# First layer of a graph network: one chunk's weighing, sums, product and statistics in one turn, and the layer's join in the same block

## The chip, the core and the metric

The kernel runs on one core of a Trainium2 chip. The metric is device time in microseconds (us), median of three runs. Engines are named as in the profile: PE (matrix products), DVE (vector), ACT (activations), POOL (here it issues the gathers), SP (issues the plain transfers). Each works through its own instructions in order and waits on semaphores for the others.

## The reference

Four graph layers follow each other on 50,000 nodes of 128 features. The change is in the first one:

```python
h = x @ W
norm = dinv[src] * dinv[dst]              # with loops added, dinv = rsqrt(degree)
out = segment_sum(h[src] * norm[:, None], dst) + b
out = layer_norm(out) * ln_gamma + ln_beta
x = _layernorm(x + relu(out))             # what the next layer starts from
```

The kernel sums the weighted rows of `x` first and multiplies the sum by `W` afterwards. The edges are sorted by `dst`, so that a node's sum is a run along the edges; the runs that cross from one partition into the next are mended at the end, in the join.

## The kernel before

The padded edges lie in 128 partitions; a chunk is 7 columns of them (7 rows of 128 features in each partition), and there are 56 chunks (`k.NB`). A chunk passes through these steps:

- `load` on SP brings its records; `fetch` (L1436) on POOL issues 14 gathers, two for each column, which bring the target's own row (`in`, `own` in the code) and the source's row (`both`).
- `weigh` (L1454) on ACT: 14 scaled copies into `run` and `summed`.
- `edges` (L1469) on DVE: 7 chained steps that carry the run along the columns (L1475), then 7 steps that add the run to `summed` (L1477).
- PE turns `summed` (L1067), ACT copies the turned rows (L1108), PE multiplies by `W` onto the bias (L1073, L1079), ACT copies the product into `z` (L1116). This goes in two groups, of 4 and 3 columns (`GROUPS`).
- `stats` on DVE: mean and variance of `z` (L780 to L776); `first.log` on ACT: Ln and Exp (L790, L792), a first guess of the inverse root; `first.root` on DVE: one Newton step (L799 to L803); `first.apply` on ACT: `z` to `y` (L811).
- `residual` (L1498) on DVE: gain, bias, relu and the row of `x` (L1501 to L1503), then the statistics of `y`; `second.log`, `second.root`, and on ACT `apply_second` (L1507), which writes two tables' rows (`out`, 14 activations, all on L811). SP stores them (L1044), and stores `run` as well (`keep`, L1481).

`Flow.run` (L1021) writes the instructions out chunk by chunk: on every engine a turn goes through a list of steps, and each step has a lag, the number of chunks by which it runs ahead of the turn's own chunk. On DVE the list is `edges` 3 ahead, `stats` 0, `residual` 1 behind, `first.root` 0, `second.root` 1 behind. On ACT it is `weigh` 4 ahead, `apply_second` 2 behind, the product of the chunk 1 ahead, both `log`, `first.apply` 0, and the copies of turned rows. POOL fetches 4 ahead and SP loads 5 ahead of the turn and stores 3 behind. All loops are written out, none runs on the chip. Before the first chunk's sums, DVE prepares the later layers' weights (`side.vector`).

After the 56 chunks this block ends with a barrier of all engines, and a second block does the join: POOL gathers three small tiles (L1546 to L1549), then one chain of sums, product and three row norms runs through DVE, PE, ACT and POOL (`RowNorm`, L1171), and POOL writes the result into both tables (L1554). Then the next layer starts.

Of the kernel before, what the change touches and what calls it, by code (L numbers as in the profile page):

```python
# [11 lines left out]
I32 = mybir.dt.int32  # L12
# [5 lines left out]
D = 128  # L18
# [1145 lines left out]
class RowNorm:  # L1164
# [9 lines left out]
    def run(self, dve, step, v, o):  # L1174
        step(dve.bn_stats(out=self.raw[:], in_=v))  # L1175
        step(dve.bn_aggr(out=self.mv[:], in_=self.raw[:]))  # L1176
        step(dve.tensor_scalar(self.mv[:, 1:2], self.mv[:, 1:2], self.eps, None, ALU.add))  # L1177
        dve.nop().then_inc(self.asked, 1)
        dve.wait_ge(self.rooted, 1)
        step(dve.tensor_scalar(o, v, self.mv[:, 0:1], self.mv[:, 1:2], ALU.subtract, ALU.mult))  # L1180
# [225 lines left out]
def gcn(k):  # L1406
# [3 lines left out]
    with ExitStack() as c:  # L1410
# [58 lines left out]
        def edges(dve, step, c):  # L1469
# [17 lines left out]

        def kept(sp):
            for u in range(RING):
                sp.wait_ge(put_out[u], k.NB // RING * 16)  # L1490
            for u in range(UB):
                sp.wait_ge(src_out[u], k.TN * 16)
# [14 lines left out]
        def apply_second(act, c):  # L1507
            n.wait_stored(act, c)
            act.wait_ge(src_out[c.slot(UB)], (c.use(UB) + 1) * 16)
            second.apply(act, c, R(y, c), R(n.o[0], c))  # L1510
            second.apply_twice(act, c, R(y, c), R(n.o[1], c))

        side = Prepare(k, c, [n.p_t[0][0], n.p_t[1][0], *n.p_m], [y, n.z, n.o[0]])

        def begin(dve):
            side.vector(dve)
            step = Chain(dve, begun)
            step(dve.memset(run[:, RING - 1, J - 1, :], 0.0))

            step(dve.memset(n.o[1][:, :, :, 0:1], 1.0))  # L1520

        n.z_free = first.applied
        n.finished, n.freed = second.applied2, sem("freed")
        n.n_got = 2
# [15 lines left out]
        with nc.Block(no_gpsimd_drain=True) as b:  # L1540

            @b.gpsimd
# [1679 lines left out]
```

## Time and profile before

| | us |
|---|---|
| median of three runs (lowest, highest) | 6258.33 (6258.26, 6266.45) |
| span of the profiled execution, first to last instruction | 6250.9 |
| what the median has over that span | 7.4 |
| the 56 chunks' first gather on POOL, last gather | 356.17, 1373.04 |
| first instruction of the join's block | 1467.26 |
| first DVE instruction of the next layer | 1488.74 |

The page gives the profiled execution's span and no other time of its own; where a time of the whole is needed, the 7.4 us between span and median stand for what lies around it. Busy shares over the whole span (PE 73%, DVE 85%, ACT 75%, POOL 61%) are means over all four layers; the first one covers about 356 to 1489 us, and only that stretch matters here.

A row of a timeline gives the start, the length, the engine, the line of the kernel, the operation, what is written and read, the count where rows are merged, and in brackets the idle time of the engine ahead of it and who ended it. Instructions of one engine overlap: the next one may start before the last has ended.

### The profile page before, as it was taken

The numbers are of one execution on the slowest core, as the hardware profiler recorded it, in microseconds if no ns is written. First come the engines' busy times: TensorE is split into PE (matmuls) and PEld (weight loads), VectorE is DVE, ScalarE is ACT, GpSimd is POOL, SyncE is SP. The second block draws the span as 40 slices with busy tenths as digits, with TensorE's granted clock in tenths as the row PEclk, the third lists the DMA queues.
The fourth block names the chain that finished last, engine by engine and source line by source line (L and its number), as shares of the span: only waits on it lengthen the run. The fifth ranks groups of instructions, "written<-read, shape, count | busy, mean of one in ns | idle before, by whom it ended". The sixth has DMA issues, their size and how long they took to land. (4 is left out here: it accounts for less than half of the span.)

```text
span 6250.9 us, 117617 instructions
## 1 busy us (share of the span) xinstructions
PE 4548.2 (73%) x28601; PEld 3543.8 (57%) x28601; DVE 5315.0 (85%) x27201; ACT 4686.9 (75%) x14259; POOL 3804.5 (61%) x3880
## 2 busy tenths in 40 slices
PE   4143333333999979999979999949996769888881
PEld 2022222222888868888856777636654557666661
DVE  8767777774999978999969999957767859999996
ACT  7017888884999978999959999945545648888884
POOL 3057777763777737666366666447753445777774
PEclk9555555556999989999989999979998989999995
DMA  9377555553888845666547676646657954444441
GB/s 191 45 66 134 133 125 133 130 126 102 240 246 248 244 156 189 206 216 205 183 144 206 198 206 203 177 143 205 208 173 255 299 179 152 151 163 152 156 158 42
DMA packets 608007, 1075.90 MB, mean 172 GB/s; under 512 B 263700, under 2 KB 370015, under 8 KB 607193
## 3 DMA queue, kind: packets, MB, share of 16 engines
q1 hardware_dynamic: 476056, 787.63, 39.5%
q0 software_dynamic: 129920, 280.46, 20.6%
q8 instruction: 231, 3.78, 0.3%
q14 instruction: 456, 3.73, 0.2%
q10 hardware_dynamic: 1344, 0.30, 0.0%
HBM read 564.38 MB, written 530.59 MB: 175 GB/s over the span
## 5 line engine op out<-in xcount | busy, mean ns | idle before, releaser
L1925 POOL DMA_INDIRECT xs<-tab,rec x1176 | 1156.7, 984 | 358.4 <-issue 318.2
L2049 ACT ACTIVATE st<-xs,cb 128x128 f32<-128x128 f32 x2352 | 814.5, 401 | 0.9 <-DVE cg L1639 0.9
L2173 DVE SCALAR_TENSOR_TENSOR st<-st,cg 128x128 f32<-128x128 f32 x2352 | 719.5, 348 | 41.3 <-ACT st L2049 36.9
L1980 PE MATMUL p_y<-w_all,xt 128*128 128x258 f32 x2352 | 722.7, 390 | 30.6 <-DVE cA L2138 29.6
L2057 ACT ACTIVATE z<-p_a 128x384 f32<-128x384 f32 x1176 | 574.0, 488 | 119.3 <-PE p_a L1817 108.1
L1448 POOL DMA_INDIRECT in<-in_x,rec x392 | 388.0, 990 | 402.0 <-DMA rec<-meta 283.2
L2138 DVE CUSTOM_DVE_ANT_0 junk<-p_y,xs 128x129 f32<-128x129 f32 x2352 | 585.9, 288 | 11.4 <-PE p_y L1980 9.6
L1073 PE MATMUL p_m<-b_rows,ones_bf 3*128 3x512 bf16 x224 | 100.0, 446 | 648.3 <-ACT z L1116 648.3
L886 ACT ACTIVATE o<-y,norm 128x127 f32<-128x127 f32 (+1 forms) x1176 | 513.7, 488 | 6.8 <-DVE norm L880 6.7
L1817 PE MATMUL p_a<-ident,st 128*128 128x128 f32 x2352 | 468.1, 281 | 67.0 <-DVE st L2173 62.9
L2757 POOL DMA_INDIRECT xs<-res,rec x392 | 388.8, 992 | 198.8 <-issue 98.8
L2040 ACT ACTIVATE xt<-p_t 128x256 f32<-128x256 f32 (+1 forms) x1221 | 448.6, 368 | 79.5 <-PE p_t L1964 77.5
L1976 PE MATMUL p_a<-w_all,xt 128*128 128x128 f32 x2352 | 479.4, 286 | 27.1 <-ACT xt L2040 26.5
L2760 POOL DMA_INDIRECT out<-o,nodes x392 | 399.9, 1020 | 154.5 <-issue 118.5
L1997 PE MATMUL p_m<-w_all,xt 128*128 128x128 f32 x2352 | 489.4, 290 | 0.0
L1923 POOL DMA_INDIRECT xd<-tab,rec x336 | 338.1, 1006 | 231.5 <-DMA rec<-meta 155.9
L1141 POOL DMA_INDIRECT in<-tab,rec x392 | 390.8, 997 | 125.3 <-issue 119.2
L1817 PEld LDWEIGHTS p_a<-ident,st 128*128 128x128 f32 x2352 | 303.2, 141 | 272.5 <-DVE st L2173 189.9
L1821 PE MATMUL p_m<-w_all,z 128*128 128x128 f32 x2352 | 455.2, 275 | 0.1
L1822 PE MATMUL p_m<-w_all,z 128*128 128x128 f32 x2352 | 454.3, 274 | 0.0
L1073 PEld LDWEIGHTS p_m<-b_rows,ones_bf 3*128 3x128 bf16 x224 | 21.2, 95 | 710.1 <-ACT z L1116 691.2
L1452 POOL DMA_INDIRECT both<-x_info,rec x336 | 330.4, 983 | 102.4 <-issue 102.4
(778 smaller groups left out, 16334.5 us busy)
## 6 DMA issues: line engine op xcount, KB each, us to landing
states<-st SPq DMA_DIRECT2D x168, 910.0 KB
own<-tab SPq DMA_DIRECT2D x168, 448.0 KB
tab<-o SPq DMA_DIRECT2D x168, 448.0 KB
runs<-run SPq DMA_DIRECT2D x112, 448.0 KB, 6.8
tab<-out SPq DMA_DIRECT2D x112, 448.0 KB
x<-tab SPq DMA_DIRECT2D x112, 448.0 KB
xd<-tab SPq DMA_DIRECT2D x168, 192.0 KB, 3.5
angles<-st SPq DMA_DIRECT2D x56, 532.0 KB
```

Of the source, the lines that this page charges most:

```text
L886: ins = act.activation(o[:, r, skip:], v[:, r, skip:], ACT.Identity, bias=s[:, 1, r : r + 1], scale=s[:, 0, r : r + 1])
L1817: ins = pe.transpose(p_a[i][:, h * D : (h + 1) * D], halves(a)[:, h, :], k.ident[:])
L1821: pe.matmul(out_, a[:, 0:D], k.w_val[:, 0, :], start=False, stop=False)
L1822: return pe.matmul(out_, a[:, D : 2 * D], k.w_val[:, 1, :], start=False, stop=final)
L1925: pool.indirect_dma_start(xs[:, i, j, 0:D], None, table, bass.IndirectOffsetOnAxis(ap=rec[:, i, SRC, j : j + 1], axis=0)).then_inc(got_in[ ...
L1976: ins = pe.matmul(p_a[two(own_c, own_i)][:, 2 * D : 3 * D], xt[:, four(c, i), D : 2 * D], k.w_own[:, D : 2 * D], start=True, stop=True)
L1980: ins = pe.matmul(p_y[two(c, i)][:, 0 : H * X1], xt[:, four(c, i), 0:D], k.w_qk[:], start=True, stop=True)
L1997: pe.matmul(out_, xt[:, (four(c, j) + SCORE * J + 1) % 4, D : 2 * D], k.w_own[:, 0:D], start=False, stop=False)
L2049: ins = act.activation(state_of(r, j)[:, h, :], xs[:, c.slot(UB), j, 0:D], ACT.Copy, scale=co.b[:, c.slot(2), h, j : j + 1])
L2057: act.activation(z[:, c.slot(2), j, :], p_a[two(c, j)][:, 0 : 3 * D], ACT.Copy).then_inc(st_copied, 1)
L2138: ins = dve.tensor_tensor_reduce(junk[:, two(c, j), h], p_y[two(c, j)][:, h * X1 : (h + 1) * X1], xs[:, c.slot(UB), j, :], scale, 0.0, ALU ...
L2173: ins = dve.scalar_tensor_tensor(mine[:, h, :], prev[:, h, :], co.g[:, c.slot(2), h, j : j + 1], mine[:, h, :], ALU.mult, ALU.add)
```

## The change

The lags go. In turn i every engine handles chunk i up to its statistics, the residual of chunk i-1 and the second norm of chunk i-2; the instructions of the layer are written out for it in a block of its own, no longer through `Flow.run`. ACT weighs chunk i first in turn i and makes its Ln and Exp last in turn i. DVE takes the sums of chunk i, the residual of i-1, the statistics of i, then the roots of i-1 (second norm) and of i (first norm). The sums are handed to PE in the two groups. SP loads 5 ahead of the turn as before, but ahead of `keep`, and stores 2 behind. POOL issues all gathers in a row. The join's instructions stand in the same block: its two gathers that need no run follow the chunks' gathers, the gather of runs waits for the stores of `run`, the join's sums come ahead of the last residual on DVE, and its writes wait for the stores of both tables. The join uses three other banks.

```diff
     def run(self, dve, step, v, o):
+        self.ask(dve, step, v)
+        self.take(dve, step, v, o)
+
+    def ask(self, dve, step, v):
         step(dve.bn_stats(out=self.raw[:], in_=v))
         step(dve.bn_aggr(out=self.mv[:], in_=self.raw[:]))
         step(dve.tensor_scalar(self.mv[:, 1:2], self.mv[:, 1:2], self.eps, None, ALU.add))
         dve.nop().then_inc(self.asked, 1)
+
+    def take(self, dve, step, v, o):
         dve.wait_ge(self.rooted, 1)
         step(dve.tensor_scalar(o, v, self.mv[:, 0:1], self.mv[:, 1:2], ALU.subtract, ALU.mult))
...
             r = c.slot(RING)
             dve.wait_ge(weighted, c.count(1, 1))
-            for j in range(J):
-                prev = run[:, r, j - 1, :] if j else run[:, (r - 1) % RING, J - 1, :]
-                step(dve.scalar_tensor_tensor(run[:, r, j, :], prev, n.field(c, SAME)[:, j : j + 1], run[:, r, j, :], ALU.mult, ALU.add))
-            dve.nop().then_inc(edged, 1)
-            step(*[dve.scalar_tensor_tensor(summed[:, r, j, :], run[:, r, j, :], n.field(c, OWN1)[:, j : j + 1], summed[:, r, j, :],
-                                            ALU.mult, ALU.add) for j in range(J)])
-            dve.nop().then_inc(n.prepped, 1)
+            for a, z_ in GROUPS:
+                for j in range(a, z_):
+                    prev = run[:, r, j - 1, :] if j else run[:, (r - 1) % RING, J - 1, :]
+                    step(dve.scalar_tensor_tensor(run[:, r, j, :], prev, n.field(c, SAME)[:, j : j + 1], run[:, r, j, :], ALU.mult, ALU.add))
+                if z_ == J:
+                    dve.nop().then_inc(edged, 1)
+                step(*[dve.scalar_tensor_tensor(summed[:, r, j, :], run[:, r, j, :], n.field(c, OWN1)[:, j : j + 1], summed[:, r, j, :],
+                                                ALU.mult, ALU.add) for j in range(a, z_)])
+                dve.nop().then_inc(n.prepped, 1)
...
-        cut = 1
-        n.run([], [], [k.res, k.tab[1]], lambda c: [R(summed, c)], [k.w_skip],
-              [(3, edges), (0, stats), (-1, residual), (0, first.root), (-1, second.root)],
-              [(4, weigh), (-2, apply_second), (0, first.log), (-1, second.log), (0, lambda act, c: first.apply(act, c, R(n.z, c), R(y, c)))],
-              [], prep=True, sp_stages=[(1, keep)], begin=begin, sp_end=kept,
-              pe_begin=side.tensor, sp_after={-4: side.bring, UB - 1: side.put_away}, fetch=fetch, bring=bring, cut=cut)
+        n.n_got, n.n_out = 2, 2
+        outs = [k.res, k.tab[1]]
+        at = lambda i: Chunk(k, i // UB, i % UB)
...
-        cleared, fetched, joined, done, summed1 = [sem(x) for x in ("cleared", "fetched", "joined", "jdone", "summed1")]
+        cleared, hinted, fetched, joined, done, summed1 = [sem(x) for x in ("cleared", "hinted", "fetched", "joined", "jdone", "summed1")]
         turned1, copied1, made1, ready, put = [sem(x) for x in ("turned1", "copied1", "made1", "ready", "put")]
-        p_j, p_t, p_z = n.p_t[0][0], n.p_t[1][0], n.p_m[0]
+        p_j, p_t, p_z = side.sets[1][0:3]
...
+                for i in range(LEAD):
+                    load(at(i))
+                    if i == 1:
+                        side.bring(sp)
+                for i in range(k.NB + 2):
+                    if i + LEAD < k.NB:
+                        load(at(i + LEAD))
+                    if i < k.NB:
+                        keep(sp, at(i))
+                    if i == UB - 1:
+                        side.put_away(sp)
+                    if i >= 2:
+                        store(at(i - 2))
...
             @b.gpsimd
             def _(pool):
+                for i in range(k.NB):
+                    fetch(pool, at(i))
                 pool.memset(head[:], 0.0).then_inc(cleared, 1)
+                pool.indirect_dma_start(mine[:], None, A["x"], bass.IndirectOffsetOnAxis(ap=k.head_node[:], axis=0)).then_inc(hinted, 16)
+                pool.indirect_dma_start(hint[:].bitcast(I32), None, k.info, bass.IndirectOffsetOnAxis(ap=k.head_node[:], axis=0)).then_inc(hinted, 16)
                 pool.wait_ge(cleared, 1)
+                for u in range(RING):
+                    pool.wait_ge(put_out[u], k.NB // RING * 16)
                 pool.indirect_dma_start(head[:], None, k.runs, bass.IndirectOffsetOnAxis(ap=k.join_row[:], axis=0),
                                         bounds_check=k.NR - 1, oob_is_err=False).then_inc(fetched, 16)
-                pool.indirect_dma_start(mine[:], None, A["x"], bass.IndirectOffsetOnAxis(ap=k.head_node[:], axis=0)).then_inc(fetched, 16)
-                pool.indirect_dma_start(hint[:].bitcast(I32), None, k.info, bass.IndirectOffsetOnAxis(ap=k.head_node[:], axis=0)).then_inc(fetched, 16)
                 for norm in norms:
                     norm.root(pool)
                 pool.wait_ge(ready, 1)
+                for u in range(RING):
+                    pool.wait_ge(n.stored[u], k.NB // RING * 16 * n.n_out)
...
+                side.tensor(pe)
+                for i in range(k.NB):
+                    for g in range(NG):
+                        turn(at(i), g)
+                    for g in range(NG):
+                        product(at(i), g)
+
+                pe.wait_ge(edged, k.NB)
                 pe.matmul(p_j[:, 0:D], k.join_t[:], run[:, RING - 1, J - 1, :], start=True, stop=True).then_inc(joined, 1)
+                pe.matmul(p_z[:, 0:D], k.ones_bf[:], k.b_rows[:, 0, :], start=True, stop=False)
                 pe.wait_ge(summed1, 1)
                 pe.transpose(p_t[:, 0:D], o[:], k.ident[:]).then_inc(turned1, 1)
-                pe.matmul(p_z[:, 0:D], k.ones_bf[:], k.b_rows[:, 0, :], start=True, stop=False)
                 pe.wait_ge(copied1, 1)
                 pe.matmul(p_z[:, 0:D], ot[:], k.w_skip[:], start=False, stop=True).then_inc(made1, 1)
 
...
+                for i in range(k.NB + 2):
+                    c0, c1, c2 = at(i), at(i - 1), at(i - 2)
+                    if c0.there:
+                        weigh(act, c0)
+                    if c1.there:
+                        first.apply(act, c1, R(n.z, c1), R(y, c1))
+                    if c0.there:
+                        carry_turned(c0, 0)
+                    if c2.there:
+                        n.wait_stored(act, c2)
+                        act.wait_ge(src_out[c2.slot(UB)], (c2.use(UB) + 1) * 16)
+                        second.apply(act, c2, R(y, c2), R(n.o[0], c2))
+                    if c0.there:
+                        carry_turned(c0, 1)
+                        for g in range(NG):
+                            carry_product(c0, g)
+                    if i == k.NB:
+                        act.wait_ge(turned1, 1)
+                        act.activation(ot[:], p_t[:, 0:D], ACT.Copy).then_inc(copied1, 1)
+                    if c2.there:
+                        second.apply_twice(act, c2, R(y, c2), R(n.o[1], c2))
+                    if c1.there:
+                        second.log(act, c1)
+                    if c0.there:
+                        first.log(act, c0)
 
...
+                for i in range(k.NB):
+                    c0, c1 = at(i), at(i - 1)
+                    stage(s_edges, c0, edges)
+                    stage(s_residual, c1, residual)
+                    stage(s_stats, c0, stats)
+                    stage(s_second, c1, second.root)
+                    stage(s_first, c0, first.root)
+
                 step = Chain(dve, done)
-                dve.wait_ge(fetched, 48)
+                final = at(k.NB - 1)
+                dve.wait_ge(hinted, 32)
                 step(dve.tensor_scalar(o[:], mine[:], dinv, None, ALU.mult))
                 dve.wait_ge(joined, 1)
                 step(dve.tensor_tensor(o[:], o[:], p_j[:, 0:D], ALU.add))
+                dve.wait_ge(fetched, 16)
                 step(dve.tensor_tensor(o[:], o[:], head[:], ALU.add))
                 step(dve.tensor_scalar(o[:], o[:], dinv, None, ALU.mult))
                 dve.nop().then_inc(summed1, 1)
+                stage(s_residual, final, residual)
                 dve.wait_ge(made1, 1)
-                norms[0].run(dve, step, p_z[:, 0:D], z[:])
+                norms[0].ask(dve, step, p_z[:, 0:D])
+                stage(s_second, final, second.root)
+                norms[0].take(dve, step, p_z[:, 0:D], z[:])
```

On ACT, two turns of the program in the middle of the layer. Before, from the end of a weighing (`run`, `summed`) to the next weighing's first instruction; `out` is the second norm's result, `guess_208` and `guess_221` are the first and the second norm's, `xt` the turned rows:

```order
L1466 ACTIVATE summed<-in_160,rec 128x128
L811 ACTIVATE out_161<-y,norm_224 128x128 x7
L811 ACTIVATE out_162<-y,norm_224 128x127 x7
L1116 ACTIVATE z<-p_m_167 128x512
L1108 ACTIVATE xt<-p_t_165 128x512
L790 ACTIVATE guess_208<-rad_207 128x7
L792 ACTIVATE guess_208<-guess_208 128x7
L790 ACTIVATE guess_221<-rad_220 128x14
L792 ACTIVATE guess_221<-guess_221 128x14
L811 ACTIVATE y<-z,norm_211 128x128 x7
L1116 ACTIVATE z<-p_m_168 128x384
L1108 ACTIVATE xt<-p_t_166 128x384
```

Now, from the end of one chunk's weighing to the start of the next:

```order
L811 ACTIVATE y<-z,norm_211 128x128 x7
L1625 ACTIVATE xt<-p_t_165 128x512
L811 ACTIVATE out_161<-y,norm_224 128x128 x7
L1625 ACTIVATE xt<-p_t_166 128x384
L1632 ACTIVATE z<-p_m_167 128x512
L1632 ACTIVATE z<-p_m_168 128x384
L811 ACTIVATE out_162<-y,norm_224 128x127 x7
L790 ACTIVATE guess_221<-rad_220 128x14
L792 ACTIVATE guess_221<-guess_221 128x14
L790 ACTIVATE guess_208<-rad_207 128x7
L792 ACTIVATE guess_208<-guess_208 128x7
L1471 ACTIVATE run<-both 128x128
```

Before, three more steps stood between the Ln and Exp and the next weighing, and the chunk weighed was four ahead of the one whose statistics were taken; now the Ln and Exp of the chunk that was weighed in this turn (`guess_208`) are the last thing ahead of the next weighing.

On DVE before, from a turn's sums (`run`, `summed`) to its residual; `raw_205` are the statistics of `z`, `raw_218` those of `y`, `ISA` clears a counter of steps:

```order
L1475 SCALAR_TENSOR_TENSOR run<-run,rec 128x128 x7
L1477 SCALAR_TENSOR_TENSOR summed<-run,rec,summed 128x128 x7
L177 ISA
L780 BN_STATS raw_205<-z 128x6 x7
L782 BN_AGGR mv_206<-raw_205 128x2 x7
L783 COPY mean_210<-mv_206 128x7
L776 TENSOR_SCALAR rad_207<-mv_206 128x7
L177 ISA
L1501 TENSOR_TENSOR y<-y,ln_g 128x896
L1502 TENSOR_TENSOR y<-y,ln_b 128x896
L1503 SCALAR_TENSOR_TENSOR y<-y,in_160 128x896
```

Now, from the second group's sums (ahead of it stand `run` x4, `summed` x4 and `run` x3) to the statistics of `z`:

```order
L1485 SCALAR_TENSOR_TENSOR summed<-run,rec,summed 128x128 x3
L177 ISA
L1503 TENSOR_TENSOR y<-y,ln_g 128x896
L1504 TENSOR_TENSOR y<-y,ln_b 128x896
L1505 SCALAR_TENSOR_TENSOR y<-y,in_160 128x896
L780 BN_STATS raw_218<-y 128x6 x7
L782 BN_AGGR mv_219<-raw_218 128x2 x7
L783 COPY mean_223<-mv_219 128x7
L776 TENSOR_SCALAR rad_220<-mv_219 128x7
L903 TENSOR_SCALAR rad_220<-mv_219 128x7
L177 ISA
L780 BN_STATS raw_205<-z 128x6 x7
```

The residual has moved ahead of the statistics of `z`, and these now belong to the chunk whose sums stand in the same turn, where they belonged to the one three chunks earlier.

## Rows read from the trace of the kernel before

**Rows 1.** Windows: stretch; PE, PEld, DVE, ACT, POOL busy; PEclk, DMA, GB/s.

```profile
452.00:1374.00 922.00, 308.36 (x1200) 229.67 (x1198) 715.96 (x3047) 739.70 (x2164) 704.51 (x714) 0.52 0.62 131
1374.00:1467.00 93.00, 19.55 (x72) 14.43 (x72) 63.68 (x286) 68.70 (x191) 0.00 (x0) 0.53 0.24 83
```

**Rows 2.** Timeline of POOL: start us, us, engine line op [idle before].

```profile
452.14 0.94 POOL L1448 DMA_INDIRECT in<-in_x,rec  x1 [7.72 <-DMA rec<-meta]
...
1373.04 0.94 POOL L1452 DMA_INDIRECT both<-x_info,rec  x1 [0.30 <-issue]
1467.26 0.20 POOL L1544 MEMSET head<- 128x128 f32 x1 [93.28 <-POOLq L1021]
...
1483.58 1.04 POOL L1554 DMA_INDIRECT res<-z,join_row  x1 [1.39 <-DVEq L1590]
```

**Rows 3.** Waits of ACT and DVE, 340 to 1500 us: total, times, longest.

```profile
ACT run L1465 <- DMA both<-x_info,rec: 102.1, 34, 7.3
...
DVE newton L799 <- ACT guess L792: 81.9, 35, 6.5
```

**Rows 4.** Timeline of DVE, one turn after the last gather.

```profile
1392.39 2.68 DVE L1475 SCALAR_TENSOR_TENSOR run<-run,rec 128x128 f32<-128x128 f32 x7 [0.34 <-DVE norm L803]
1395.22 1.93 DVE L1477 SCALAR_TENSOR_TENSOR summed<-run,rec,summed 128x128 f32<-128x128 f32 x7
1397.47 1.45 DVE L780 BATCH_NORM_STATS2 raw<-z 128x6 f32<-128x128 f32 x7 [0.33 <-DVE summed L1477]
...
1399.65 0.16 DVE L776 TENSOR_SCALAR rad<-mv 128x7 f32<-128x7 f32 x1
1400.14 1.09 DVE L1501 TENSOR_TENSOR y<-y,ln_g 128x896 f32<-128x896 f32 x1 [0.33 <-DVE rad L776]
...
1405.88 0.16 DVE L903 TENSOR_SCALAR rad<-mv 128x7 f32<-128x7 f32 x1
1406.37 0.17 DVE L799 TENSOR_TENSOR newton<-guess 128x7 f32<-128x7 f32 x1 [0.33 <-DVE rad L903]
...
1407.68 0.17 DVE L799 TENSOR_TENSOR newton<-guess 128x14 f32<-128x14 f32 x1 [0.33 <-DVE norm L803]
```

**Rows 5.** Timeline of ACT, first and last instruction of one weighing.

```profile
927.16 0.39 ACT L1465 ACTIVATE run<-both 128x128 f32<-128x128 f32 x1
...
930.96 0.39 ACT L1466 ACTIVATE summed<-in,rec 128x128 f32<-128x128 f32 x1
```

**Rows 6.** Timeline of ACT, the same turn as rows 4.

```profile
1406.13 0.21 ACT L790 ACTIVATE guess<-rad 128x14 f32<-128x14 f32 x1 [5.10 <-DVEq L784]
1406.38 0.21 ACT L792 ACTIVATE guess<-guess 128x14 f32<-128x14 f32 x1
1407.44 2.80 ACT L811 ACTIVATE y<-z,norm 128x128 f32<-128x128 f32 x7 [0.85 <-DVEq L805]
1410.14 0.47 ACT L1116 ACTIVATE z<-p_m 128x384 f32<-128x384 f32 x1
```

**Rows 7.** Timeline of PE: bias, four products, four transposes; later three products.

```profile
1400.27 0.60 PE L1073 MATMUL p_m<-b_rows,ones_bf 3*128 3x512 bf16 x1 [3.52 <-ACT z L1116]
1400.80 2.08 PE L1079 MATMUL p_m<-w_all,xt 128*128 128x128 f32 x8
1402.67 1.06 PE L1067 MATMUL p_t<-ident,summed 128*128 128x128 f32 x4
...
1411.09 1.65 PE L1079 MATMUL p_m<-w_all,xt 128*128 128x128 f32 x6
```

**Rows 8.** Timeline of DVE, first sums of the layer; first work after it.

```profile
441.62 2.68 DVE L1475 SCALAR_TENSOR_TENSOR run<-run,rec 128x128 f32<-128x128 f32 x7
...
1488.74 0.27 DVE L2112 MEMSET b_block<- 12x256 uint32 x1 [6.04 <-PEq L123]
```

**Rows 9.** Timeline of ACT, the last chunk's two norms.

```profile
1457.47 5.48 ACT L811 ACTIVATE out<-y,norm 128x128 f32<-128x128 f32 x14 [1.22 <-DVEq L805]
```

**Rows 10.** Page, section 6: the table of runs, KB each, us to landing.

```profile
runs<-run SPq DMA_DIRECT2D x112, 448.0 KB, 6.8
```

More of the change, by code:

```diff
@@ L1486, in keep @@
                 sp.dma_start(k.meta[:, c.n, SRC, :], where[:, c.slot(UB), :, 0].bitcast(I32)).then_inc(src_out[c.slot(UB)], 16)
[L1488 to L1492, printed above, removed]
         def stats(dve, step, c):
@@ L1539, in gcn, with _, load, store @@
         dinv = hint[:, 1:2]
         with nc.Block(no_gpsimd_drain=True) as b:
+            @b.sync
+            def _(sp):
+                def load(c):
+                    wait(sp, n.freed, c.count(1, 1 - UB), n.passed)
+                    sp.dma_start(n.rec[:, c.slot(UB)].rearrange("p f j -> p (f j)"),
+                                 k.meta[:, c.n].rearrange("p f j -> p (f j)")).then_inc(n.rec_in[c.slot(UB)], 16)
+                    bring(sp, c)
+                def store(c):
+                    wait(sp, n.finished, c.count(1, 1), n.passed)
+                    for i, table in enumerate(outs):
+                        sp.dma_start(rows(table)[:, c.n, :],
+                                     n.o[i][:, c.slot(RING)].rearrange("p j d -> p (j d)")).then_inc(n.stored[c.slot(RING)], 16)
+                for i in range(LEAD):
[12 more added lines that the diff above has]
+                for u in range(RING):
+                    sp.wait_ge(n.stored[u], k.NB // RING * 16 * n.n_out)
+                    sp.wait_ge(put_out[u], k.NB // RING * 16)
+                for u in range(UB):
+                    sp.wait_ge(src_out[u], k.TN * 16)
@@ L1552, in _ @@
                 pool.wait_ge(ready, 1)
+                for u in range(RING):
+                    pool.wait_ge(n.stored[u], k.NB // RING * 16 * n.n_out)
                 for table, tile in ((k.res, z), (k.tab[1], o)):
@@ L1559, in _, with turn, product @@
             def _(pe):
+                def turn(c, g):
+                    a, z_ = GROUPS[g]
+                    pe.wait_ge(n.prepped, c.count(NG, g + 1))
+                    wait(pe, n.copied, c.count(NG, g - 1))
+                    for r in range(a, z_):
+                        ins = pe.transpose(n.p_t[g][0][:, (r - a) * D : (r - a + 1) * D], R(summed, c)[:, r, :], k.ident[:])
+                    ins.then_inc(n.turned, 1)
+                def product(c, g):
+                    a, z_ = GROUPS[g]
+                    wait(pe, n.z_in, c.count(NG, g - 1))
+                    pe.matmul(n.p_m[g][:, 0 : (z_ - a) * D], k.ones_bf[:], k.b_rows[:, 0 : z_ - a, :].rearrange("p r d -> p (r d)"),
+                              start=True, stop=False)
+                    pe.wait_ge(n.copied, c.count(NG, g + 1))
+                    for r in range(z_ - a):
+                        ins = pe.matmul(n.p_m[g][:, r * D : (r + 1) * D], n.xt[:, g, 0, r * D : (r + 1) * D], k.w_skip[:], start=False,
+                                        stop=r == z_ - a - 1)
+                    ins.then_inc(n.made, 1)
+                side.tensor(pe)
[5 more added lines that the diff above has]
+                pe.wait_ge(edged, k.NB)
                 pe.matmul(p_j[:, 0:D], k.join_t[:], run[:, RING - 1, J - 1, :], start=True, stop=True).then_inc(joined, 1)
+                pe.matmul(p_z[:, 0:D], k.ones_bf[:], k.b_rows[:, 0, :], start=True, stop=False)
                 pe.wait_ge(summed1, 1)
                 pe.transpose(p_t[:, 0:D], o[:], k.ident[:]).then_inc(turned1, 1)
-                pe.matmul(p_z[:, 0:D], k.ones_bf[:], k.b_rows[:, 0, :], start=True, stop=False)
                 pe.wait_ge(copied1, 1)
@@ L1568, in _, with carry_turned @@
             def _(act):
-                act.wait_ge(turned1, 1)
-                act.activation(ot[:], p_t[:, 0:D], ACT.Copy).then_inc(copied1, 1)
+                act.preload_act_table_set("natural_log_exp_and_others")
+                def carry_turned(c, g):
+                    a, z_ = GROUPS[g]
+                    act.wait_ge(n.turned, c.count(NG, g + 1))
+                    wait(act, n.made, c.count(NG, g - 1))
+                    act.activation(n.xt[:, g, 0, 0 : (z_ - a) * D], n.p_t[g][0][:, 0 : (z_ - a) * D], ACT.Copy).then_inc(n.copied, 1)
@@ new lines, in carry_product @@
+                def carry_product(c, g):
+                    a, z_ = GROUPS[g]
+                    act.wait_ge(n.made, c.count(NG, g + 1))
+                    if g == 0:
+                        wait(act, n.z_free, c.count(1, 1 - RING))
+                    act.activation(n.z[:, c.slot(RING), a:z_, :].rearrange("p j d -> p (j d)"),
+                                   n.p_m[g][:, 0 : (z_ - a) * D], ACT.Copy).then_inc(n.z_in, 1)
+                for i in range(k.NB + 2):
[23 more added lines that the diff above has]
+                        first.log(act, c0)
@@ L1572, in _, with stage @@
             @b.vector
             def _(dve):
+                side.vector(dve)
+                begin = Chain(dve, begun)
+                begin(dve.memset(run[:, RING - 1, J - 1, :], 0.0))
+                begin(dve.memset(n.o[1][:, :, :, 0:1], 1.0))
+                s_edges, s_residual, s_stats, s_second, s_first = [
+                    Steps(dve, sem(x), n.passed) for x in ("d_edges", "d_residual", "d_stats", "d_second", "d_first")]
+                def stage(step, c, what):
+                    if c.there:
+                        step.at(c)
+                        what(dve, step, c)
+                        step.end()
```

11 lines of the change are left out of this document (removed).

## The prediction

> **What bounds the kernel now.** I read the windows of the first layer first, then POOL's timeline, the waits, and one turn of DVE, ACT and PE. From 452 to 1374 us POOL makes 714 gathers that are busy 704.51 us, and behind each it needs 0.30 us to issue the next: 714 x 0.30 is 214 us, and the two fill the 922 us [rows 1, 2]. So POOL is solid, and a chunk of 14 gathers takes (1373.04 - 452.14) / 713 x 14 = 18.08 us. ACT and DVE keep up: ACT waits 102.1 us for gathered rows, DVE 81.9 us for ACT's guess [rows 3]. DVE's own turn is 5.08 us of sums (1392.39 to 1397.47), 2.67 of statistics, 6.23 of residual (1400.14 to 1406.37) and two roots of 1.31, together 16.6 us [rows 4], under the 18.08. Then comes a tail: after the last gather POOL has nothing for 93.28 us [rows 2], in which DVE and ACT are still busy 63.68 and 68.70 us [rows 1], because the steps of a chunk are spread over seven turns. The join follows behind a barrier, from 1467.26 to the next layer's first DVE instruction at 1488.74 [rows 2, 8].
>
> **The change part by part.** What goes: most of the tail, the barrier, and the join's place behind it. At the start nothing moves: DVE's preparation ends where the first sums begin, 441.62 [rows 8]. SP now loads a chunk's records ahead of the store of runs, so POOL's one pause of 7.72 us [rows 2] goes.
>
> What comes: a chain inside each turn. DVE can't sum chunk i before ACT has weighed it; ACT weighs it only after the Ln and Exp of chunk i-1; these need DVE's statistics of i-1, and those stand on DVE behind the sums of i-1 and the residual of i-2. Before, lags of 4 and 3 turns cut this chain. Its length:
> - weighing, 927.16 to 930.96 + 0.39: 4.19 us [rows 5];
> - hand-over from ACT to DVE 0.1, taken from the 0.09 between DVE's last output (1405.88 + 0.16) and ACT's Ln at 1406.13 [rows 4, 6];
> - sums, 5.08 us before, now in two groups: the change from the chain to the sums to PE, 1395.22 - (1392.39 + 2.68) = 0.15, comes once more, and the independent sums (1.93 / 7 = 0.28 apart) lose their overlap once, 0.1: 5.3 us [rows 4];
> - residual 6.23; statistics to the last output, 1397.47 to 1399.65 + 0.16, 2.34 [rows 4];
> - hand-over 0.09, Ln to Exp 0.25, Exp 0.2 before the next weighing starts behind five waits [rows 6].
>
> The sum is 4.19 + 0.1 + 5.3 + 6.23 + 2.34 + 0.09 + 0.25 + 0.2 = 18.7 us a turn, against the 18.08 of the gathers. The roots (2 x 1.31) lie beside the next weighing's 4.19 and cost nothing as long as that covers them.
>
> One term of it is not in the trace, the split of the sums. It could cost nothing, if the second chain follows as closely as the steps within one (2.68 / 7 = 0.38 us apart), or 0.5 us, if each of the change-overs costs more like the 0.33 us between DVE's steps [rows 4]. The chained steps with a wait behind each stand 0.38 us apart, the independent ones without a wait 0.28; so a wait costs here, and I take the 0.25 us worked out above, nearest to the 0.15 of the row; 18.45 and 18.95 us a turn are the ends. The Trainium skill ("VectorE: DVE Perf Modes", section "The DRAIN you can't avoid") says that a semaphore behind each vector instruction takes no more time than one behind the last. This trace differs, with 0.38 beside 0.28; by that rule the split is free, the turn 18.45 us, and the time 54 x 0.25 = 13.5 us below the one forecast here, 6268.
>
> Does the product come back in time? From the weighing's start: first group's sums at 4.3 + 2.8 = 7.1, four transposes 1.06 [rows 7], ACT's copy at 8.2 to 8.7 (weighing and a norm, 4.1 + 2.7, are done at 6.8 [rows 5, 6]), a norm 2.7 to 11.4, the second copy 0.4 to 11.8; PE, free at about 10.2, needs 0.53 + 2.08 for the first product, then 0.4 + 1.65 for the second: 12.9 and 14.9 [rows 7]; copies to 15.3; norm to 18.0; the second norm's Ln and Exp, 0.35, to 18.4. DVE has its residual done at 15.8, after z is there, and its statistics at 18.2. So the two chains are level within 0.2 us; if ACT's is the later, the turn is 18.85. That lies within the ends above, and I take 18.7.
>
> The whole layer: sums of chunk 0 start at 441.62; its product is back 5.0 + 0.1 + 0.8 + 0.5 + 2.1 + 0.4 + 1.7 + 0.5 = 11.1 us later, at 452.7, and 2.34 + 0.09 + 0.25 + 0.2 later ACT starts weighing chunk 1: 455.6. POOL is then four chunks ahead and stays there. 54 turns of 18.7 bring chunk 55 to 1465.4, its turn's end to 1484.1. Then, one behind the other: the last roots, 2.1, to 1486.2; first norm 0.1 + 2.8 [rows 6], 1489.1; residual 0.1 + 5.9, 1495.1; Ln and Exp 0.6, 1495.7; the join's statistics 0.7 and the root 1.1, 1497.5; both tables 0.1 + 5.48 [rows 9], 1503.1. From the end of these (1457.47 + 5.48 = 1462.95) to the next block took 4.31 us [rows 2, 9], here the stores' landing: 1507.4; from the join's first write to the next layer 1488.74 - 1483.58 = 5.16 [rows 2, 8]: 1512.5. The next layer starts 23.8 us later than at 1488.74.
>
> The join itself costs nothing more: its gather of runs waits for the last store of runs, started some 9 us into turn 55, at 1474, and 6.8 us in landing [rows 10], and its sums stand on DVE behind the last roots; its three norms run beside ACT's last 5.48 us and the stores. Without that cover it would be the 16.3 us from 1467.26 to 1483.58 [rows 2]. The later layers are the same instructions. Span 6250.9 plus the 7.4 us around it plus 23.8: 6282.
>
> **The rivals.**
>
> The gathers go on setting the pace, and the change gives its tail back. For it: POOL is the one solid engine [rows 1, 2]. Against it: the chain above holds no gather at all. The point is the turn's length: at 18.08 the last chunk starts 54 x 0.62 = 33.5 us sooner, 9.7 us faster than before, 6249. If ACT, DVE and PE could follow the last gather at once, with the 7.72 us pause gone it ends at 1366.3, is there 6.8 us later by the landing of rows 10, and the 47.1 us from the last weighing to the next layer end at 1420: 68.6 us faster, 6190. Break-even is a turn of 18.7 - 23.8 / 54 = 18.26.
>
> The product comes back late. If PE and ACT take half a microsecond more on the way (a later transpose, a copy queued behind a norm), DVE waits at the statistics of every turn, since z arrives only 0.5 us ahead of the residual's end and ACT's chain has no room at all: 54 x 0.5 = 27 us more, 6309. For it: everything in a turn is now one chunk's work, with no other chunk to fill in. Against it: PE is idle most of the stage, 308.36 of 922 us busy [rows 1].
>
> The chain is a little shorter than summed (hand-overs nearer zero, waits hidden behind the Exp): a turn of 18.2 to 18.45, 6255 to 6268. For it: several terms were rounded up.
>
> **How the numbers follow.** The summed chain has 0.65: 6282, with 18.45 to 18.95 us a turn 6268 to 6296. The gathers' pace or near it 0.17, the late product 0.10, the shorter chain 0.08. About 0.2% (12.5 us) is what a measurement of this kernel can tell from no change. Faster by more than that is most of the gathers' case, 0.13; the same are its rest, the shorter chain and a little of the main case, 0.15; slower the main case and the late product, 0.72. The range, 6247 to 6309, leaves out the gathers' case below 6247 and what goes beyond the late product's half microsecond.
>
> **What would show it.** Right: POOL pauses for records between chunks instead of running solid; ACT starts each weighing right behind the first norm's Exp, 18.5 to 18.9 us apart; DVE waits 1.5 to 2 us for the weighing in each turn, and hardly for z; the next layer starts near 1512. Wrong: weighings that start on gathered rows, 18.1 us or less apart (the gathers' case), or DVE's statistics waiting for z in each turn (the late product). A difference in the later layers would be none of these.

## The result, and the profile after

| | us |
|---|---|
| after, median of 10 runs (lowest, highest) | 6278.96 (6274.22, 6280.52) |
| before, 10 runs beside them | 6266.01 (6258.26, 6273.27) |
| ratio after to before, 95% interval | 1.0021 (1.0012 to 1.0030) |
| profiled execution of after: its time, its span | 6278.74, 6276.3 |

The changed kernel is slower, by 0.21% (0.12 to 0.30%). The forecast was 6282 us, slower than before by 23.8 us; the two medians differ by 13.

The first layer by windows (columns as in [rows 1]), of after:

```profile
452.00:1374.00 922.00, 325.07 (x1143) 225.98 (x1142) 694.62 (x2951) 727.70 (x2097) 680.27 (x691) 0.52 0.59 125
1374.00:1467.00 93.00, 32.83 (x115) 22.75 (x115) 69.95 (x292) 73.68 (x213) 18.79 (x21) 0.50 0.30 89
```

Against [rows 1], every engine gets through fewer instructions in the first 922 us: POOL has 691 gathers in it where it had 714, DVE 694.62 us of work where it had 715.96. (Only PE's busy time is longer, 325.07 against 308.36 us, for fewer instructions; no run here shows why.) The work is the same, so it is spread thinner. No engine is solid now: the busiest, ACT, has 727.70 of 922 us. This points to a chain across engines, which the experiments test. The waits of after, 340 to 1520 us (as [rows 3]):

```profile
POOL in L1454 <- DMA rec<-meta: 313.4, 35, 271.6
...
ACT z L1632 <- PE p_m L1598: 134.9, 112, 2.0
DVE run L1482 <- ACT summed L1472: 113.8, 55, 3.1
...
ACT run L1471 <- DMA both<-info,rec: 28.4, 1, 28.4
...
DVE raw L780 <- ACT z L1632: 6.4, 2, 6.1
```

ACT's 34 waits for gathered rows [rows 3] are gone: the one left, 28.4 us, is ahead of the first chunk. In their place DVE waits once in each of 55 turns for the weighing, 2.07 us on average, and POOL, which had one pause of 7.72 us [rows 2], now waits for records between chunks (313.4 less the 271.6 before the layer is 41.8 us in 34 waits). For `z` DVE hardly waits. One turn on DVE, after:

```profile
911.85 1.51 DVE L1482 SCALAR_TENSOR_TENSOR run<-run,rec 128x128 f32<-128x128 f32 x4 [2.08 <-ACT summed L1472]
913.40 1.14 DVE L1485 SCALAR_TENSOR_TENSOR summed<-run,rec,summed 128x128 f32<-128x128 f32 x4
914.69 1.13 DVE L1482 SCALAR_TENSOR_TENSOR run<-run,rec 128x128 f32<-128x128 f32 x3
915.97 0.88 DVE L1485 SCALAR_TENSOR_TENSOR summed<-run,rec,summed 128x128 f32<-128x128 f32 x3
917.17 1.09 DVE L1503 TENSOR_TENSOR y<-y,ln_g 128x896 f32<-128x896 f32 x1 [0.33 <-DVE summed L1485]
...
923.40 1.45 DVE L780 BATCH_NORM_STATS2 raw<-z 128x6 f32<-128x128 f32 x7 [0.33 <-DVE rad L903]
...
925.58 0.16 DVE L776 TENSOR_SCALAR rad<-mv 128x7 f32<-128x7 f32 x1
926.07 0.17 DVE L799 TENSOR_TENSOR newton<-guess 128x14 f32<-128x14 f32 x1 [0.33 <-ACT guess L792]
```

And the same turn on ACT, from one weighing's start to the next:

```profile
907.62 0.40 ACT L1471 ACTIVATE run<-both 128x128 f32<-128x128 f32 x1
...
911.73 2.78 ACT L811 ACTIVATE y<-z,norm 128x128 f32<-128x128 f32 x7
915.81 0.60 ACT L1625 ACTIVATE xt<-p_t 128x512 f32<-128x512 f32 x1 [1.30 <-PE p_t L1588]
...
920.43 0.60 ACT L1632 ACTIVATE z<-p_m 128x512 f32<-128x512 f32 x1 [0.97 <-PE p_m L1598]
922.44 0.49 ACT L1632 ACTIVATE z<-p_m 128x384 f32<-128x384 f32 x1 [1.41 <-PE p_m L1598]
...
925.87 0.19 ACT L790 ACTIVATE guess<-rad 128x7 f32<-128x7 f32 x1
926.09 0.21 ACT L792 ACTIVATE guess<-guess 128x7 f32<-128x7 f32 x1
926.26 0.40 ACT L1471 ACTIVATE run<-both 128x128 f32<-128x128 f32 x1
```

Read them together: weighing from 907.62; sums 911.85 to 917.17; residual to 923.40; statistics, last output 925.74; Ln 925.87, Exp, next weighing 926.26. That is the forecast chain without a gap, 18.64 us. On ACT, the first copy of turned rows and both copies into `z` wait for PE, and yet DVE's statistics start only 0.33 us behind its own last step. From the last `z` on ACT works without a pause, and its Ln starts 0.13 us behind DVE's last output and 0.12 behind the start of its own Exp before it: the way of the product through ACT and DVE's own way are level.

The two ends of the layer on DVE, first sums and next layer's first work ([rows 8]), of after:

```profile
445.46 1.51 DVE L1482 SCALAR_TENSOR_TENSOR run<-run,rec 128x128 f32<-128x128 f32 x4
...
1515.55 0.27 DVE L2227 MEMSET b_block<- 12x256 uint32 x1 [10.13 <-PEq L123]
```

On ACT, chunk 55's weighing and the last second norm ([rows 9]), of after:

```profile
1468.30 0.40 ACT L1471 ACTIVATE run<-both 128x128 f32<-128x128 f32 x1
...
1500.33 5.49 ACT L811 ACTIVATE out<-y,norm 128x128 f32<-128x128 f32 x14 [1.82 <-DVEq L805]
```

On POOL, the last chunk's last gather, the join's gather of runs and its first write ([rows 2]), of after:

```profile
1394.92 0.95 POOL L1458 DMA_INDIRECT both<-x_info,rec  x1 [0.30 <-issue]
...
1480.14 1.01 POOL L1569 DMA_INDIRECT head<-runs,join_row  x1 [81.70 <-DMA runs<-run]
...
1510.34 1.06 POOL L1577 DMA_INDIRECT res<-z,join_row  x1 [5.43 <-DMA tab<-out]
```

The next layer starts 1515.55 - 1488.74 = 26.8 us later than in [rows 8], and the span is 25.4 us longer: the later layers differ by 1.4 us. Of the 26.8 us, 3.8 lie ahead of the first sums and 23.0 in the layer itself. That difference hides two larger ones. The last chunk's sums on DVE, of after (before they stand at 1392.39 [rows 4]):

```profile
1472.53 1.51 DVE L1482 SCALAR_TENSOR_TENSOR run<-run,rec 128x128 f32<-128x128 f32 x4 [2.10 <-ACT summed L1472]
```

From the layer's first sums to these it took 950.8 us before and takes 1027.1 now; from these to the next layer it took 96.4 us and takes 43.0. So the end of the layer gave back 53.3 us and the 55 turns cost 76.3. Before, a turn took 17.29 us on average, less than the gathers' 18.08, as the first gather started 85 us ahead of the first sums and gathered chunks lay ready: ACT waits for rows in 34 of these turns only [rows 3].

### The profile page after: what moved, and what is told of

Read it like the earlier page. It is cut to its first block and busy times, and to the rows that moved or that the text cites. A ratio compares the mean times of both kernels' runs of the same rounds, so it can differ in the third digit from the quotient of the medians.

```text
span 6276.3 us, 117719 instructions
## 1 busy us (share of the span) xinstructions
PE 4586.8 (73%) x28601; PEld 3554.6 (57%) x28601; DVE 5315.0 (85%) x27201; ACT 4699.1 (75%) x14259; POOL 3800.6 (61%) x3880
## 5 line engine op out<-in xcount | busy, mean ns | idle before, releaser
L1454 POOL DMA_INDIRECT in<-in_x,rec x392 | 392.1, 1000 | 422.2 <-DMA rec<-meta 313.4
L1588 PE MATMUL p_t<-ident,summed 128*128 128x128 f32 x392 | 113.0, 436 | 675.4 <-DVEq L1487 675.4
L1588 PEld LDWEIGHTS p_t<-ident,summed 128*128 128x128 f32 x392 | 68.2, 215 | 713.8 <-DVEq L1487 705.8
L2112 PEld LDWEIGHTS p_m<-w_all,xt 128*128 128x128 f32 x2352 | 354.0, 190 | 67.8 <-issue 67.8
```

The lines of the kernel that those rows point to most:

```text
L2112: pe.matmul(out_, xt[:, (four(c, j) + SCORE * J + 1) % 4, D : 2 * D], k.w_own[:, 0:D], start=False, stop=False)
```

## The experiments

Times are medians against the kernel before on the same chip. As the first sums start at 439 to 446 us from one execution to the next, I compare traces by the time from the first sums to the next layer's first DVE instruction: 1047.1 us before (1053.6 in a second trace of it, so some 6 us of any difference from before can be scatter), 1070.1 us after. The ratio of the changed kernel itself, to set beside those below, is 1.0021.

**Who sets the pace.** One of the 14 gathers a chunk is left out, in either kernel; zeros stand in its place, and ACT waits for 13. The same edit in before, in after, and (below) in a third kernel:

```diff
             for j in range(J):
...
-                pool.indirect_dma_start(own[:, i, j, :], None, A["x"], mine).then_inc(n.got[i], 16)
+                if j < J - 1:
+                    pool.indirect_dma_start(own[:, i, j, :], None, A["x"], mine).then_inc(n.got[i], 16)
```

> The kernel before with 13 gathers a chunk instead of 14: the target's own row of the last column is left out (zeros stand for it, so the result of these columns is another). If the gathers set its pace: 13 x 1.29 = 16.8 us a chunk, near DVE's 16.6, 51 x 1.2 = 60 us faster (50 to 66), 6205. If not: no change.

Measured: 6195.97 against 6255.09 us, ratio 0.9902 (0.9886 to 0.9919). From the first sums to the next layer (440.10 to 1427.72) it takes 987.6 us, 59.5 less. The gathers set the pace before.

> The changed kernel with the same gather left out. Chain theory: no gather in the chain, 6279 within 3 us, the turn still 18.6 to 18.7. If gathers set its pace: 54 x 1.25 = 67 us faster, 6212.

Measured: 6271.73 against 6255.09, 1.0026 (1.0016 to 1.0036); first sums to next layer (439.21 to 1507.97) 1068.8 us where after had 1070.1. The time is 7 us below the 6279 of the expectation, and 6.25 of them are the earlier first sums (445.46 in the trace of after). A fourteenth less of gathers changes nothing in the turns: no gather is in the chain of after.

**How much of before's time is its own scatter.** The kernel before, unchanged:

> The kernel before, unchanged, for a second trace of it. Its ten times reach from 6258 to 6273 us, the changed kernel's from 6274 to 6281. If the spread lies in the gathers' pace (each of the 714 takes 1.25 to 1.9 us), a trace with a longer span has its next layer start later than 1488.74 us by about as much as the span is longer than 6250.9, and a pace above 18.08 us a chunk; the changed kernel, which doesn't wait for gathers, would not have it. If the spread lies in the later layers, the next layer starts at 1489 within 2 us whatever the span.

Measured: 6257.07 against 6260.24, 0.9997 (0.9988 to 1.0006). Its profiled execution took 6259.79 for a span of 6258.1. The last gather on POOL, kernel before run again:

```profile
1378.37 0.94 POOL L1452 DMA_INDIRECT both<-x_info,rec  x1 [0.30 <-issue]
```

In [rows 2] it stands at 1373.04. The next layer started at 1495.03, 6.3 us after [rows 8], in a span 7.2 us longer. So the trace of before that I had worked from was one of the shorter executions, and these two differ in the gathers' pace.

**The tail alone.** Two lags of before one smaller, everything else as before:

```diff
-              [(3, edges), (0, stats), (-1, residual), (0, first.root), (-1, second.root)],
-              [(4, weigh), (-2, apply_second), (0, first.log), (-1, second.log), (0, lambda act, c: first.apply(act, c, R(n.z, c), R(y, c)))],
+              [(2, edges), (0, stats), (-1, residual), (0, first.root), (-1, second.root)],
+              [(3, weigh), (-2, apply_second), (0, first.log), (-1, second.log), (0, lambda act, c: first.apply(act, c, R(n.z, c), R(y, c)))],
```

> The kernel before with two lags shorter by one: sums 2 chunks ahead instead of 3, weighing 3 instead of 4. If the tail behind the last gather is the number of turns by which a chunk is spread, at 13.2 us a turn (1407.44 to 1420.62), and the pace stays the gathers': 13 us faster, 6253. If a shorter lag already makes a chain in the turn as in the changed kernel: not faster, or slower.

Measured: 6239.02 against 6255.09, 0.9969 (0.9957 to 0.9982), 16 us where 13 were expected; first sums to next layer 1031.7 us, 15.4 less than before. The last gather starts at 1374.85, as late as before, and from it to the next layer it takes 99.4 us instead of 115.7. One turn less of lag is about one turn less of tail, as long as the chain stays open: this small edit is faster than before, where the whole change is slower.

**The join alone.** After, with the join in a block of its own behind a barrier again (its instructions are moved as they are; one wait of PE goes, which the barrier covers):

```diff
+                stage(s_residual, final, residual)
+                stage(s_second, final, second.root)
+
+        with nc.Block(no_gpsimd_drain=True) as b:
...
                 dve.nop().then_inc(summed1, 1)
-                stage(s_residual, final, residual)
                 dve.wait_ge(made1, 1)
                 norms[0].ask(dve, step, p_z[:, 0:D])
-                stage(s_second, final, second.root)
```

> The changed kernel with the join's instructions in a block of their own again, behind a barrier. If the join is hidden beside the last chunk's norms and stores: it comes back with the 21.5 us that it had from its first instruction to the next layer, less the 5.2 us that the last writes take in either place and some 1 us on the last chunk's path: 15 us slower than the changed kernel (12 to 18), 6294. If it costs as much in the same block: within 3 us of 6279.

Measured: 6293.69 against 6260.24, 1.0055 (1.0040 to 1.0071). From the first sums to the next layer it takes 1525.87 - 441.4 = 1084.5 us, 14.4 more than after. Putting the join into the block is worth 14.4 us; the longer turns eat it.

**The split of the sums.** After, with the sums in one group:

```diff
-            for a, z_ in GROUPS:
-                for j in range(a, z_):
...
-                dve.nop().then_inc(n.prepped, 1)
+            for j in range(J):
...
+            dve.nop().then_inc(n.prepped, NG)
```

> The changed kernel with the sums of a chunk in one group again: 7 chained steps, 7 sums, and only then both groups go to PE. If DVE's chain alone sets the turn and the split costs 0.25 us of it: 0.25 x 54 = 13.5 us faster than the changed kernel, 6265. If the way of the product through PE and ACT is level with it, as worked out in the prediction: the first group's transposes start 2.3 us later in a turn, ACT's chain gets about 1.1 us longer (19.8 us from weighing to weighing), 54 x 1.1 = 60 us slower, 6340. If the split costs nothing on DVE and the product has room: 6279.

Measured: 6309.56 against 6260.24, 1.0080 (1.0065 to 1.0095); first sums to next layer 1547.52 - 441.55 = 1106.0, 35.9 more than after. DVE of the one-group kernel, the steps around one turn:

```profile
916.32 1.46 DVE L780 BATCH_NORM_STATS2 raw<-z 128x6 f32<-128x128 f32 x7 [0.96 <-ACT z L1630]
...
923.84 2.67 DVE L1481 SCALAR_TENSOR_TENSOR run<-run,rec 128x128 f32<-128x128 f32 x7 [1.99 <-ACT summed L1472]
926.66 1.93 DVE L1483 SCALAR_TENSOR_TENSOR summed<-run,rec,summed 128x128 f32<-128x128 f32 x7
```

The sums take 928.91 - 923.84 = 5.07 us here, 5.32 in after: the split costs DVE 0.25. But PE starts on the first group later without it, and in this turn DVE waits 0.96 us for `z`, 0.63 more than the 0.33 between its own steps. The turn is 19.3 us on average, 0.65 longer. This is the late product of the rivals, with 0.65 us a turn where 0.5 stood there. The expectation for this case, 60 us slower than after, was twice the 30.6 measured: over 53 turns the first copy of turned rows starts 2.07 us later behind the weighing's start (8.19 in after, 10.26 here), but the last `z` is there only 0.69 us later (15.31 and 16.00), as ACT's waits for products shrink from 134.9 to 67.0 us.

**The link cut.** After, with ACT weighing chunk i+1 in turn i, so that sums no longer wait for the Exp of the chunk before; the second copy of turned rows moves ahead as well:

```diff
+                weigh(act, at(0))
                 for i in range(k.NB + 2):
                     c0, c1, c2 = at(i), at(i - 1), at(i - 2)
-                    if c0.there:
-                        weigh(act, c0)
                     if c1.there:
                         first.apply(act, c1, R(n.z, c1), R(y, c1))
+                    if i + 1 < k.NB:
+                        weigh(act, at(i + 1))
                     if c0.there:
                         carry_turned(c0, 0)
+                        carry_turned(c0, 1)
...
-                        carry_turned(c0, 1)
```

> The changed kernel with one step moved on ACT: chunk i+1 is weighed in turn i, behind the first norm of chunk i-1, and no longer at the head of turn i+1; the second copy of turned rows moves ahead of the second norm's first table. Chain theory (the turn is weighing, sums, residual, statistics, Ln and Exp, one behind the other): the 4.2 us of weighing leave the chain, DVE's turn is then 5.3 + 6.2 + 2.7 + 2.6 = 16.9 to 17.3 us, under the gathers' 18.1, so gathers set the pace and the tail behind the last one is short: the next layer's first DVE instruction comes near 1430 instead of 1515.55 us, the time is 6195 to 6215. Rival (the work of a turn on ACT and DVE makes it 18.6 us long, in whatever order): within 10 us of the changed kernel's 6279. Rival (gathers set the pace of the changed kernel): no change either.

Measured: 6217.14 against 6260.24, 0.9929 (0.9916 to 0.9943); first sums to next layer (442.57 to 1451.55) 1009.0 us, 61.1 less than after. How much of it belongs to the moved copy alone was not tested. The turn is 17.56 us, not the gathers' 18.08. I had taken the gathers for the next bound; the waits of this kernel speak against that:

```profile
ACT y L811 <- DVEq L805: 123.3, 56, 2.5
...
DVE newton L799 <- ACT guess L792: 36.7, 55, 0.7
DVE raw L780 <- ACT z L1632: 35.3, 55, 6.1
...
ACT run L1471 <- DMA both<-info,rec: 25.1, 1, 25.1
```

ACT waits for a gather once, before the first chunk. The sums start 442.6 - 356.1 = 86.5 us, nearly five chunks, behind the first gather, and at 17.56 against 18.08 us they gain only 29 us on the gathers in 55 turns. Whether gathers or DVE decide, 13 gathers tell apart:

> Weighing one chunk ahead in the changed kernel, and 13 gathers a chunk as above. If weighing ahead is then bound by gathers at 18.1 us a chunk, 13 of them allow 16.8 and DVE's turn, 16.9 to 17.3, comes next: 50 x 0.8 to 1.2 = 40 to 60 us faster than weighing ahead with 14 gathers. If weighing ahead is bound by the work of ACT and DVE: no change between the two.

Measured: 6210.61 against 6255.09, 0.9925 (0.9909 to 0.9942), where the link cut alone gave 0.9929: no gain. So the gathers are not the bound. What is left, it seems, is DVE's own chain with its two small waits for ACT in each turn. Then those waits must be worth something. The edit, against after:

```diff
+                    if ahead:
+                        weigh(act, ahead)
...
+                    if ahead:
+                        weigh_some(act, ahead, 3, 5)
+                    if c0.there:
+                        carry_product(c0, 0)
+                    if ahead:
+                        weigh_some(act, ahead, 5, J)
+                    if c0.there:
+                        carry_product(c0, 1)
...
+                    if c1.there and c0.there:
+                        second.log(act, c1)
                     if c2.there:
                         second.apply_twice(act, c2, R(y, c2), R(n.o[1], c2))
```

Here `weigh` takes the columns 0 to 2 and `weigh_some` the rest; the second copy of turned rows stands where after has it.

> weigh_ahead with the weighing of the next chunk cut in three pieces, each put where VectorE waited there (columns 0 to 2 ahead of the second norm's apply, 3 and 4 ahead of the first group of z, 5 and 6 ahead of the second), and the second norm's Ln ahead of its apply. In weigh_ahead a turn is 17.56 us and VectorE waited in each for ScalarE's z (0.35 us or more) and for the root's first guess (0.35 us). If VectorE's own chain is what is left (13 gathers did not shorten weigh_ahead), the turn falls to about 16.95 us, 55 turns save some 33 us, until the gathers, which end near 1370 us of the span, are level with it: about 6187 us, 1.1 to 1.2 per cent under the kernel before. Rival: the waits come back at other places of the turn (ScalarE's two further starts, 0.2 us each, are then late for VectorE), the turn stays at 17.4 to 17.6 and the time at 6210 to 6220. A second rival: the gathers now set the pace, the turn is 17.3 or more at the end with VectorE waiting through ScalarE for a DMA, 6195 to 6210.

Measured: 6197.85 against 6259.27, 0.9898 (0.9881 to 0.9914), the fastest kernel of the study with all of the computation in it. DVE's first sums of a chunk and its statistics, at two places of this kernel's timeline:

```profile
963.54 1.51 DVE L1488 SCALAR_TENSOR_TENSOR run<-run,rec 128x128 f32<-128x128 f32 x4 [0.34 <-DVE norm L803]
...
975.12 1.46 DVE L780 BATCH_NORM_STATS2 raw<-z 128x6 f32<-128x128 f32 x7 [0.33 <-DVE rad L903]
...
980.46 1.51 DVE L1488 SCALAR_TENSOR_TENSOR run<-run,rec 128x128 f32<-128x128 f32 x4 [0.34 <-DVE norm L803]
...
1313.33 1.45 DVE L780 BATCH_NORM_STATS2 raw<-z 128x6 f32<-128x128 f32 x7 [1.78 <-ACT z L1638]
...
1318.68 1.53 DVE L1488 SCALAR_TENSOR_TENSOR run<-run,rec 128x128 f32<-128x128 f32 x4 [0.34 <-DVE norm L803]
...
1331.73 1.45 DVE L780 BATCH_NORM_STATS2 raw<-z 128x6 f32<-128x128 f32 x7 [1.82 <-ACT z L1638]
...
1337.07 1.51 DVE L1488 SCALAR_TENSOR_TENSOR run<-run,rec 128x128 f32<-128x128 f32 x4 [0.34 <-DVE norm L803]
```

And its waits from 1120 to 1400 us:

```profile
ACT run L1476 <- DMA both<-x_info,rec: 26.6, 15, 1.9
DVE raw L780 <- ACT z L1638: 25.2, 15, 1.8
```

The first theory of the expectation holds at first, its second rival at the end. At first a turn is 980.46 - 963.54 = 16.92 us with DVE waiting for nobody; so the sums catch up with the gathers, and after some 40 turns ACT finds its rows not yet there, DVE waits 1.8 us for `z`, and the turn is 1337.07 - 1318.68 = 18.39 us. That ended at 6198, inside the 6195 to 6210 of that rival and some 11 us behind the 6187 that the first theory gave.

## Why the prediction was right

Its steps, and what stands in their place (us):

| step | forecast | measured |
|---|---|---|
| turn, weighing to weighing | 18.7 | 18.64; over 54 turns 18.68 |
| sums in two groups | 5.3 | 5.32 |
| first copy of turned rows, last `z`, from the weighing's start | 8.2, 15.3 | 8.2, 15.3 |
| first sums of the layer | 441.62 | 445.46 |
| weighing of chunk 55 | 1465.4 | 1468.3 |
| from there to the next layer | 47.1 | 47.25 |
| next layer's start against before | +23.8 | +26.8 |
| around the span | 7.4 | 2.4 |

*The chain is the bound.* Shown: the gathers' number does not matter in after, and weighing one chunk ahead, which cuts the link from the Exp to the next chunk's sums, takes 61.1 us away (with the second copy of turned rows moved too). The chain's length came out within 0.06 us of the sum.

*The split.* Its 0.25 us was worked out from the change-over of [rows 4], and the one-group kernel measured 0.25. The rule of the Trainium skill ("VectorE: DVE Perf Modes", section "The DRAIN you can't avoid"), by which a semaphore behind each instruction costs nothing and the split would have been free, does not hold for this pair of kernels.

*The two chains level within 0.2 us.* Shown from both sides. In after DVE hardly waits for `z`, and ACT waits for the first norm's `rad` in 4 of 56 turns, two of them at the start. In 34 of the 56, ACT's Ln starts within 0.10 us behind DVE's last output; in the other 22 it starts later than that, 0.12 to 0.13 us behind the start of ACT's own Exp before it. So which of the two ways closes the loop changes from turn to turn. And a last `z` that came 0.69 us later in the turn (one group) made the turn 0.65 longer, although DVE's sums had become shorter.

*The join hidden.* Shown by 14.4 us where 16.3 stood as the price without cover. The gather of runs stood at 1480.14 where 1480.8 followed from the terms, but that is luck, as two of these were off and cancelled: the last store of runs starts later than the 1474 assumed, behind the run's end at 1475.37 + 1.13 (the layer itself had started later), and the page has 3.0 us for its landing where [rows 10] had 6.8:

```profile
runs<-run SPq DMA_DIRECT2D x112, 448.0 KB, 3.0
```

*The start.* "At the start nothing moves" was wrong by 3.84 us in this execution, but not by the change: over the traces of all kernels here the first sums start between 439.0 and 445.5, and in after PE waited 74.6 us for a DMA of the preparation where it had waited 69.8 before.

*What lies around the span.* This term was mis-sized. I set one execution's span beside the median of others and called the 7.4 us between them surroundings. In executions that have both numbers these are 1.7 to 2.9 us; so the execution of before that was traced took about 6253, some 5 us less than the median given. That the time came out 3 us from the forecast is therefore in part luck: +3.0 for the next layer's start, -1.4 for the later layers and -5.0 for the surroundings of the span make the difference between 6282 and 6279. The change itself was forecast at +23.8 us. Trace against trace the layer takes 23.0 us more, but the medians differ by 13 only, as the traced execution of before was a short one. Before follows the gathers, and its ten times scatter over 15 us; after follows a chain without them, and its ten scatter over 6. That the scatter of before is the gathers', only one pair of its traces shows, for a difference of 7 us.

*The rivals.* The gathers' pace is excluded by the kernels with 13 gathers; the late product did not occur in after, but its mechanism is real (one group). The shorter chain did not come either: from chunk 2 on no turn between two weighings was under 18.6 us. Break-even at a turn of 18.26 was not put to a test at that length; the kernels on both sides of it, 17.56 and 18.64, fell on the sides it gives.

What stays open: why the gathers' pace in before differs between executions, and how much of the last kernel's 6198 us its late waits for gathers cost.

## What to carry to other kernels

Before taking lags out of a pipeline, write down the loop that closes when a turn's last step must precede the next turn's first, and add its durations; it can be longer than any engine's work (18.64 us here, with 16.6 of it on DVE) and no total in the old kernel's profile shows it. A lag of one at one link, here the weighing, opened it and kept the short tail: 42.9 us from the last sums to the next layer, 43.0 without that lag and 96.4 before. And test who sets the pace by taking away a little of its work: a fourteenth of the gathers was worth 59.5 us in one kernel and 1.3 in the other.

## What the runs showed of the hardware

Vector steps cost more than their busy time, by amounts that single rows of a trace give away. Between chained steps of 128x128, each of which needs the one before it, 0.38 us pass from start to start, between independent ones 0.28. Between two stages of the work (sums, residual, statistics, roots) DVE is idle for 0.33 us in nearly every turn. Splitting a run of 7 + 7 steps into 4 + 4 and 3 + 3 cost 0.25 us.

A gather costs POOL about 1.25 us in most cases, whoever waits for it (0.94 busy, 0.30 to the next issue), but a chunk of 14 took 18.1 us in before and 18.4 at the end of the last kernel, where 14 x 1.25 is 17.5: some 6 to 8 in 100 of the gathers are busy for more than 1.2 us, up to 1.86.
